# Spreading the y hats of a deformable convolution through DRAM instead of from SBUF

## What is computed

```
value = x @ vp_w + vp_b                       # 8 groups of 8 channels
py = base_y + ky + offset[..., 1]             # 9 taps per pixel and group
px = base_x + kx + offset[..., 0]
sampled = bilinear(value, py, px)             # zero outside the image
out = einsum('nhwgkc,nhwgk->nhwgc', sampled, mask) @ op_w
```

## Time and profile before

| | us |
|---|---|
| median of three runs | 465.24 (464.5 to 465.62) |
| the profiled execution | 465.35 |
| its span | 463.5 |
| conv stage, first product of DVE to last | 34.14 to about 259 |
| busy: PE, DVE, ACT, POOL | 411.4, 337.9, 258.5, 141.0 |
| DMAs of `a_rep` | 128 of 256 KB, 32 of 128 KB |

### The profile page before, as it was taken

The page is one execution under the profiler, slowest core; times in us unless marked ns, Lnnn a source line. Parts: engine busy times, 40 slices in busy tenths (PEclk is TensorE's granted clock), DMA queues, the critical chain, the costliest instruction groups (busy, mean ns, idle before and its releaser), DMA issues. The chain is left out here.

```text
span 463.5 us, 9728 instructions
## 1 busy us (share of the span) xinstructions
PE 411.4 (89%) x3276; PEld 232.7 (50%) x3276; DVE 337.9 (73%) x733; ACT 258.5 (56%) x568; POOL 141.0 (30%) x172
## 2 busy tenths in 40 slices
PE   0649999999999999999998447989999999999995
PEld 0523344343543434434331235867676777777663
DVE  3475987879878798787889545769687776868652
ACT  2633663656636566465630055476767677676752
POOL 2342323224232342223300145123232423323322
PEclk9976999999999999999999755699999999999998
DMA  8078792966829578294780150000000000000000
GB/s 253 4 164 226 165 227 66 222 159 161 227 61 226 147 165 235 54 230 131 179 232 1 45 228 0 2 0 2 2 0 13 1 1 13 1 2 1 11 3 11
DMA packets 28409, 44.91 MB, mean 97 GB/s; under 512 B 6864, under 2 KB 11088, under 8 KB 27984
## 3 DMA queue, kind: packets, MB, share of 16 engines
q1 hardware_dynamic: 28368, 44.39, 37.7%
HBM read 6.11 MB, written 0.52 MB: 14 GB/s over the span
## 5 line engine op out<-in xcount | busy, mean ns | idle before, releaser
L641 DVE TENSOR_TENSOR prod<-ps_t,a_rep 128x1024 f32<-128x1024 f32 x128 | 151.9, 1218 | 38.8 <-PE ps_t L351 37.9
L351 PE MATMUL ps_t<-b,vt 32*128 32x512 f32 x512 | 74.9, 655 | 7.5 <-DVE mask L678 5.6
L746 POOL TENSOR_TENSOR a<-a,mask 128x512 f32<-128x512 f32 (+1 forms) x40 | 46.8, 1169 | 85.0 <-ACT a L507 80.9
L371 PE MATMUL ps_d<-prod,keep 128*32 128x512 f32 x512 | 68.9, 610 | 0.3
L1200 POOL TENSOR_TENSOR total<-total,share 128x256 f32<-128x256 f32 x56 | 40.8, 729 | 87.4 <-DVE share L1094 87.0
L301 PEld LDWEIGHTS ps_m<-om_r,sel 128*128 128x128 f32 x192 | 28.9, 188 | 75.3 <-ACT mask L486 28.2
L1078 DVE TENSOR_TENSOR hidden<-ps_h,gated 128x256 f32<-128x256 f32 x128 | 51.4, 415 | 4.1 <-ACT gated L1293 2.4
L1293 ACT ACTIVATE gated<-ps_h 128x256 f32<-128x256 f32 x128 | 47.9, 388 | 7.5 <-PE ps_h L1413 1.1
L301 PE MATMUL ps_m<-om_r,sel 128*128 128x256 f32 x192 | 49.2, 334 | 0.0
L1094 DVE TENSOR_TENSOR share<-ps_yf,factor 128x256 f32<-128x256 f32 x56 | 23.7, 423 | 30.7 <-ACT factor L1287 13.1
L1413 PE MATMUL ps_h<-xf,w_h 128*128 128x256 f32 x128 | 43.7, 342 | 2.0 <-ACT gated L1293 2.0
(11 more groups left out here) (150 smaller groups left out, 674.5 us busy)
## 6 DMA issues: line engine op xcount, KB each, us to landing
a_rep<-a SPq DMA_DIRECT2D x128, 256.0 KB, 4.7
a_rep<-a SPq DMA_DIRECT2D x32, 128.0 KB
w_f<-in_w SPq DMA_DIRECT2D x2, 1024.0 KB, 5.8
start<-in_start SPq DMA_DIRECT2D x1, 1344.0 KB, 7.9
x_turned<-in_x_turned SPq DMA_DIRECT2D x1, 512.0 KB, 3.7
t_tok<-in_x SPq DMA_DIRECT2D x1, 512.0 KB, 9.7
w<-in_w SPq DMA_DIRECT2D x1, 512.0 KB, 7.6
select_f<-in_select SPq DMA_DIRECT2D x1, 512.0 KB, 8.4
```

The lines of the kernel that those rows point to most:

```text
L351: mm = pe.matmul(out, vt[par][r, v % 2, :, :, :].rearrange("p j y c -> p (j y c)"), b[par][r, pair_taps(v // 2), :].rearrange("p t x -> p ...
L371: mm = pe.matmul(ps_d[r, :], fold[:, v % 2, :], p, start=v == 0, stop=False, skip_group_check=True)
L641: dve.tensor_tensor(p[:, :, :], t[:, :, :], a_rep[par][:, ms, pair_taps(v // 2), :].rearrange("p m t x -> p m (t x)"), ALU.mult).then_inc( ...
L746: pool.tensor_tensor(v, v, mask[(PAIRS * par + k) % 2][:, 0:wide, :], ALU.mult).then_inc(a_done, 1)
```

## The change

An internal DRAM tensor `board` is added, twice the size of one image's y hats (by parity). For each tap pair, SyncE waits for `a_done`, stores the pair from `a` to `board` with one DMA over 128 partitions, waits until it has landed (`a_out[k]`), and then issues the four spreading DMAs, which read `board` instead of `a`. They keep their size, number, destination and semaphore. ACT waits for `a_out[k]` instead of `a_filled[k]` before it overwrites a pair of `a`. SyncE's loop over images 2 to 7 is written out.

```
@@ -176,6 +176,7 @@
+        a_out = [sem(f"a_out{k}") for k in range(PAIRS)]
@@ -183,6 +184,7 @@
+        board = nc.dram_tensor("hats", (2, P, TAPS * PIX), F32, kind="Internal").ap()
@@ -231,18 +233,19 @@
                 for k in range(PAIRS):
+                    cols = slice(PIX * pair_taps(k).start, PIX * pair_taps(k).stop)
                     sp.wait_ge(a_done, PAIRS * n + k + 1)
+                    sp.dma_start(board[par, :, cols], a[:, pair_taps(k), :].rearrange("p t x -> p (t x)"))\
+                      .then_inc(a_out[k], 16)
+                    sp.wait_ge(a_out[k], 16 * (n + 1))
                     for m in range(DUOS):
-                        src = a[32 * m:32 * m + 32, pair_taps(k), :]
-                        sp.dma_start(a_rep[par][:, m, pair_taps(k), :],
-                                     src.unsqueeze(1).broadcast_to([32, 4, src.shape[1], PIX]))\
+                        src = board[par, 32 * m:32 * m + 32, cols]
+                        sp.dma_start(a_rep[par][:, m, pair_taps(k), :].rearrange("p t x -> p (t x)"),
+                                     src.unsqueeze(1).broadcast_to([32, 4, src.shape[1]]))\
                           .then_inc(a_filled[k], 16)
 
-            fill(0, 0)
-            fill(1, 1)
-            with sp.Fori(1, IMAGES // 2) as it:
-                for par in range(2):
-                    fill(2 * it + par, par)
+            for n in range(IMAGES):
+                fill(n, n % 2)
@@ -487,7 +490,7 @@
                 if kind == Y and positive(n):
-                    act.wait_ge(a_filled[k], 16 * DUOS * n)
+                    act.wait_ge(a_out[k], 16 * n)
```

## The result

The changed kernel takes 504.8 us (median of four runs, 503.97 to 505.25) against 464.87 before (four runs, 464.13 to 465.62): a ratio of 1.0857, 95% interval 1.0833 to 1.0881. It is slower by 39.9 us, and outside the predicted range. The profiled execution spans 502.8 us. Token stage and start are unchanged: the weights' loads are issued at 302.25 where they were at 263.74, so 38.5 us of the 39.3 that the span grew are in the convolution.

What follows compares the result with a forecast made beforehand. TensorE was taken to bound the kernel at 28.5 us per image; F = 22.5T + 5B = 17.1 + 9.75 = 26.9 us stays hidden, so 465.3 us was forecast, unchanged, with a full range of 464.0 to 492.

Steps and rivals of the forecast that it cites:

- F: Time SyncE and the DMA rings need for one image's hats: forecast 26.9 us, against 21.4 before and 28.5 available.
- the edge at 28.9: Largest per-image spreading time, in us, at which image 7's last copy still reaches DVE when needed, at 256.92.
- the rule: Above 28.9 us per image, the kernel's end moves by 8F - 231.3 us.
- the moved ACT wait: ACT's wait before overwriting `a`, moved from the broadcasts' landing to the store's: claimed to cost and gain nothing.
- The bubble, B: Ring gap from the store's last byte to the broadcast's first: 0.44 + 0.1 + 1.4 = 1.95 us per pair.
- P = 4T + T + B: Time of one tap pair, four broadcasts, one store and the bubble: 5 x 0.76 + 1.95 = 5.75 us.
- T: Time of one 262,144-byte broadcast from DRAM, used for the store too: 0.76 us, from `x_turned`'s 343 GB/s.
- the first: Rival: broadcasts hardly faster from DRAM; decides from T = 0.85 us; 483 at 0.95, 519 at 1.15; chance 0.18.
- Issue pace: Rival: SyncE's four issues keep taking 3.95 us; F = 29.7, kernel 6.3 us longer, 471.6; chance 0.14.
- Late receipt: Rival: the store lands late under load; decides from B = 2.36 us; kernel 497, or near 469; chance 0.10.
- hidden: Likeliest case: spreading grows by 5.5 us per image but stays within TensorE's 28.5; time unchanged, 464.4 to 466.2; chance 0.50.
- Theory E: From the experiments, not the prediction: the DMA engines drift apart in any such queue of 2 KB rows.

Runs made afterwards that it cites:

- the reads without a chain: Changed kernel without its stores and SyncE's wait, broadcasts reading an input in DRAM: 464.12 us, ratio 0.9977.
- own rows: Changed kernel, stores and waits kept, each broadcast reading 128 different rows of a DRAM input instead of 32 rows four times: 488.06 us, ratio 1.0486.
- other rows: Changed kernel, stores and waits kept, broadcasts reading 32 rows four times each from an input instead of the rows just stored: 506.46 us, ratio 1.0882.
- 8 KB: Changed kernel storing 16 columns of a pair instead of 512, wait kept, broadcasts reading an input: 473.99 us, ratio 1.0182.
- the chain from SBUF: Changed kernel with store and SyncE's wait kept, but broadcasts reading `a` in SBUF and ACT waiting for them as before: 552.92 us, ratio 1.1885.
- eight broadcasts in a stream: Changed kernel with only pair 2's store moved ahead of pair 1's broadcasts: 473.26 us, ratio 1.0167.

## Why the prediction was wrong

- *What bounds the kernel, and what must break:* right. TensorE sets the pace; the question is F against 28.5, and the edge at 28.9. The runs follow the rule from there within 4 us, and all that end below or just at the edge take 464 to 465.5.
- *Unrolling, the moved ACT wait, the store's bytes:* each costs nothing, as said (runs with the loop alone, with the store but no wait and, for the moved wait as the change has it, with the store one pair ahead). In the changed kernel ACT did wait for stores, 2.2 us in three waits, because the chain had become late.
- *The bubble, B:* nearly right: 1.67 in the mean of 40 for 1.95, the error on the harmless side. The lone store landed in 2.0 for 2.1.
- *The broadcasts' mean rate:* right while all engines have work: 313 to 343 GB/s for 343. At the 0.84 us of 313 GB/s F would be 22.5 x 0.84 + 5 x 1.67 = 27.3, still hidden. The 358 GB/s that the prediction also names is passed by a row it shows, 400.
- *"P = 4T + T + B" with T = 0.76:* this is the term that failed. Right in form, it was mis-sized: in a chain that waits for a landing, T isn't the mean rate of the rings but the pace of the last of 16 engines, 1.09 us in the group shown and 1.13 over the run where I had 0.76. The longer T adds 22.5 x 0.37 = 8.3 us to an image, the shorter bubble takes 1.4 away: F = 33.8 in place of 26.9, with 33.6 read from the stores. The margin to 28.9 was 2.0 us.
- *Why it could be seen before:* the row I took T from is a load with further loads queued behind it, and its window of 1.5 us is cut out of the middle. Even so its landing is late against it: 3.7 us, less the 1.35 ahead, 1.53 of bytes and 0.44 behind, leaves 0.4 us that I didn't follow up.
- *The rivals:* the first had the right place, point and price: the point from which it decides is T = 0.85, and with the F of 33.6 that was measured the rule gives 37.5 us longer. But it was put down to slow reads from DRAM, which the reads without a chain disprove, and I capped the range at T = 1.0. Issue pace: wrong, in the chain four issues and the next store start 0.55 to 0.65 us apart with no stretching. Late receipt: wrong, 0.33 us from the end of the last row (40.33) to the last step (40.66) behind a queue, and 0.34 for the store alone (25.93 to 26.27). The prediction cites the Trainium skill for this rival (DMA: Bandwidth & Descriptors, "Anatomy of one DMA — SWDGE (gpsimd) path"): some 2.0 us fixed per DMA, most of it the write's receipt. The section is on DMAs issued from GpSimd. The trace does not agree: SyncE's store alone takes 2.0 us with its bytes, 0.34 of them behind the last row, and the first store from POOL's queue has 0.36 behind it.
- *The chances:* "hidden" at 0.50 rested on a margin of 7%, with T from rows of another size, of a load that nobody in the stretch waits for. Three rivals leaned the same way; the range should have reached T = 1.15, which was the other bound of my own row, 519 us.

What stays open is why single rows take up to 0.92 us in the group shown, and up to 1.77 in the run, where most take 0.08; whether these rows are all of the lag; and whether it is always the same engines that lag. It isn't the fourfold reading (own rows), not the written rows (other rows), not the store (8 KB), and the chain from SBUF has such an end as well. Theory E is what is left, and only in part shown: no run changes the size of the rows, so that it matters isn't shown.

## What to carry to other kernels

A DMA that was waited for cost the time of its last engine here, and of everything queued before it in the same rings; a time worked out from the mean GB/s of a stream's middle was only the lower bound. So when a step is split into "store, wait, read back", issue the next store ahead of the current reads, or from another queue: here either took the cost from 40 us to nothing, with the same bytes moved. And when the forecast is "hidden", count how much of the slack is left, and take the range from the unfavourable end of each term together.

## What was not expected of the hardware

- A group of five 256 KB transfers moved at 313 GB/s for 3.4 us and then needed 1.6 us more with 0.40 to 0.07 of the engines; with eight broadcasts in a stream two pairs needed 10.0 us instead of 14.4. In that group 35 of 640 rows took over 0.15 us where most took 0.08; in a store alone none did.
- Spreading 32 rows over 128 partitions ran at 343 GB/s from DRAM where it ran at 228 from SBUF. That is in keeping with the 8 of 16 ports of the Trainium skill (SBUF — State Buffer, "Door 1: The DMA port swizzle"), which the prediction cites; but 228 is above the 218 GB/s that the page gives, and no run here parts the ports from other causes.
- SyncE was held 0.60 us by a broadcast with fourfold rows and 0.43 us by one of the same bytes with 128 rows of its own.
